# Attention probabilities left unscaled: row sums from a ones column of the values, spread by a matmul, and new orders on three engines

## The chip, the cores and the metric

The kernel runs on 1 NeuronCore of one Trainium2 chip. The metric is the device time of one execution in microseconds (us).

## The reference, cut to what matters

Four small transformer blocks act on one image of 16 x 16 = 256 tokens with 192 channels: three relative-position attention blocks (numbers 0, 1, 2), one causal attention block (number 3), and five mixture-of-experts blocks between and behind them. Each attention has 12 heads of 16 channels. Block 0, cut:

```python
attn = einsum('bnqd,bnkd->bnqk', q * scale, k) + rel_h[..., None] + rel_w[..., None, :]
attn = softmax(attn, axis=-1)                      # 12 heads x 256 queries x 256 keys
out = einsum('bnqk,bnkd->bnqd', attn, v)           # 16 channels a head
return einsum('bhwc,oc->bhwo', out, proj_w) + proj_b
```

Block 3 has no relative positions and a causal mask: the first 128 queries see only the first 128 keys.

## The kernel before

Five engines run their own written-out lists of instructions; semaphores alone join them, and each engine executes its list strictly in order. The blocks follow each other (`BLOCKS`); every block waits for the one before it, since each works on the whole of `x`.

In an attention block (`attn(n)` on each engine) TensorE first makes queries, keys and values. In blocks 0 to 2 the relative-position products go to DRAM and come back gathered (`rel`), and VectorE copies them into `q_st`. TensorE then transposes `k_st` (line 743) and `q_st` (line 760); between the two stand some matmuls on constant data, `stay_warm` (line 672), whose result nobody reads.

The heads then go in six pairs, p = 0 to 5. This is the pair loop:
- `scores(p)` (TensorE, line 777) writes two heads' 256 x 256 scores into two PSUM banks. There are two sets of banks, so pair p uses those of pair p - 2.
- `row_max(p)` (VectorE, line 1196; in block 3 a mask is added first and lines 1189 and 1192 take its place) makes the negated row maxima, one instruction a head.
- `exps(p)` (ScalarE, line 537) writes exp(score - max) to `probs`, two instructions a head, each with a row sum as a second output (`accum_out`).
- `recip(p, h)` (VectorE, line 1200) inverts the row sums, 2 numbers per partition.
- GpSimd (line 432) multiplies `probs` of one head, 128 x 512, by them. The very first head of a block is scaled by VectorE instead (line 1207).
- `probs_transposed(p)` (TensorE, line 805) makes 8 transposes into two banks; ScalarE copies one (line 550), VectorE the other (line 1218), to `pT`.
- For each of three groups of four heads, `values_summed(g)` (TensorE, line 817) multiplies by the values `v_st`, whose heads are padded from 16 to 32 columns with zeros; ScalarE copies the result to `oT` (line 544), and `project(g)` (line 786) applies the output projection.

When the last projection is done VectorE adds the result to `x` (line 1226), and the layer norm of the next block begins. TensorE's order of scores, transposes, value sums and projections is a loop over p, as are ScalarE's and VectorE's.

```python
                        for t in range(TT):
                            act.activation(probs[:, p % 2, h, t, 0:keys_of(n, t)], scores_bank(p, h)[:, t, 0:keys_of(n, t)], ACT.Exp,
                                           bias=nmax[:, p % 2, h, t:t + 1],
                                           accum_out=rsum[:, p % 2, h, t:t + 1]).then_inc(exp_ready, 1)
```

Of the kernel before, what the change touches and what calls it, by code (L numbers as in the profile page):

```python
# [13 lines left out]
P = 128  # L14
SIDE = 16
T = SIDE * SIDE
TT = T // P
# [56 lines left out]
def metaformer_kernel(nc, a, out):  # L74

    ctx = ExitStack()
    with ctx:
# [36 lines left out]
        yplace = sb("yplace", [P, C])  # L114
        nmax = sb("nmax", [P, 2, 2, TT])
        rsum = sb("rsum", [P, 2, 2, TT])
        rinv = sb("rinv", [P, 2, 2, TT])
# [90 lines left out]
        rinv_ready, p_ready, p_ready_dve = sem("rinv_ready"), sem("probs_ready"), sem("probs_ready_dve")  # L208
# [188 lines left out]
        def _(pool):  # L397
# [10 lines left out]
            pool.memset(v_st[:, :, :, :], 0.0).then_inc(pool_ready, 1)  # L408
# [12 lines left out]
            def attn(n):  # L421
                if not ATTN[n]["rel"]:


                    pool.wait_ge(qT_psum, 3 * n)
                    pool.memset(q_st[:, :, :, HD:HD + 2 * SIDE], 0.0).then_inc(q_clear, 1)
                for p in range(PAIRS):
                    g = n * PAIRS + p
                    for h in range(1 if p == 0 else 0, 2):
                        pool.wait_ge(rinv_ready, 2 * g + h + 1)  # L430
                        pr = probs[:, p % 2, h]
                        pool.tensor_tensor(pr, pr, rinv[:, p % 2, h].unsqueeze(2).broadcast_to([P, TT, T]), ALU.mult).then_inc(p_ready, 1)  # L432
# [56 lines left out]
        def _(act):  # L489
# [19 lines left out]
            def attn(n):  # L509
# [7 lines left out]
                if n == 0:  # L517
                    act.wait_ge(pool_ready, 4)
# [14 lines left out]
                def exps(p):  # L533
                    for h in range(2):
                        act.wait_ge(nmax_ready, 2 * (n * PAIRS + p) + h + 1)
                        for t in range(TT):
                            act.activation(probs[:, p % 2, h, t, 0:keys_of(n, t)], scores_bank(p, h)[:, t, 0:keys_of(n, t)], ACT.Exp,  # L537
                                           bias=nmax[:, p % 2, h, t:t + 1],
                                           accum_out=rsum[:, p % 2, h, t:t + 1]).then_inc(exp_ready, 1)

                def outputs(g):

                    act.wait_ge(o_psum, n * GROUPS + g + 1)
                    act.activation(oT[:, g, :], bank[B_O[g]][:, 0:T], ACT.Copy).then_inc(o_ready, 1)
# [3 lines left out]
                for p in range(PAIRS):  # L548
                    act.wait_ge(pT_psum, n * PAIRS + p + 1)
                    act.activation(pT[:, p % 3, 0].rearrange("p h t -> p (h t)"), bank[B_PT[0]][:, :], ACT.Copy).then_inc(pT_act, 1)  # L550
                    if p + 2 < PAIRS:
                        exps(p + 2)
                    if p and p % 2 == 0:
                        outputs(p // 2 - 1)
                outputs(GROUPS - 1)
# [96 lines left out]
        def _(pe):  # L652
# [21 lines left out]
            def attn(n, k):  # L674
# [73 lines left out]
                stay_warm(3 if n < 3 else 0, B_V)  # L748
# [15 lines left out]
                def scores(p):  # L764
# [7 lines left out]
                    if p == 4:  # L772
                        pe.wait_ge(qT_act, 2 * n + 2)

# [18 lines left out]
                def probs_transposed(p):  # L793
# [4 lines left out]
                    for h in range(2):  # L798
                        if p == 0 and h == 0:
                            pe.wait_ge(p_ready_dve, n + 1)  # L800
                        else:
                            pe.wait_ge(p_ready, (2 * PAIRS - 1) * n + 2 * p + h)
# [18 lines left out]

                pe.wait_ge(qT_dve, n + 1)
                stay_warm(2 if n == 3 else 1, B_PT[0])

                for p in range(PAIRS):
                    if p == 0:
                        probs_transposed(0)
                        scores(2)
                        pe.wait_ge(qT_act, 2 * n + 2)
                        continue  # L830
                    if p + 2 < PAIRS:
                        pe.wait_ge(p_ready, (2 * PAIRS - 1) * n + 2 * p + 1)
                        scores(p + 2)
                    probs_transposed(p)
                    if p % 2 == 0:
                        values_summed(p // 2 - 1)
                    if p == PAIRS - 2:
# [672 lines left out]
```

## Time and profile before

| | |
|---|---|
| time, median of 3 runs | 487.48 us (485.43 to 493.93) |
| the profiled execution | 492.98 us |
| span of its trace, first to last instruction | 491.1 us |
| TensorE busy | 439.6 us, 90% |
| VectorE busy | 339.2 us, 69% |
| ScalarE busy | 234.6 us, 48% |
| GpSimd busy | 173.5 us, 35% |
| mean granted TensorE clock | 0.983 of 2.4 GHz |

PE is TensorE, DVE is VectorE, ACT is ScalarE, POOL is GpSimd. The profiled execution is 1.9 us longer than its span. Busy shares are over the whole kernel, most of which is expert blocks; what an edit of the attention is worth must be read from the stretches of the four pair loops. A row gives start and duration in us (durations marked ns are nanoseconds), the engine, the line of the kernel, and, in brackets, how long the engine stood idle before it and what ended that. TensorE's matmuls overlap, so the distance between two starts is what one costs, not its duration. A 32-bit matmul shows as two records. A row of windows has the stretch, its length, the busy us of PE, PEld (weight loads), DVE, ACT and POOL, each with its count, then the granted clock, the DMA share and GB/s.

### The profile page before, as it was taken

What the parts mean: (1) busy time and instruction counts of PE and PEld (TensorE: products, weight loads), DVE (VectorE), ACT (ScalarE), POOL (GpSimd) and SP (SyncE); (2) the same over time, 40 slices, a digit from 0 to 9 for tenths busy, and PEclk for the clock granted to TensorE, in tenths of its full rate; (3) what the DMA queues carried; (4) which work ended last, traced back from release to release, by engine and by line L of the source; (5) the groups of instructions that cost most, each with busy time, mean ns of one, the idle gap of its engine ahead of it and who ended that gap; (6) DMA issues with size and microseconds to landing.
All of it is one profiled execution on the core that took longest, in us unless ns stands there. A gap on an engine that the chain in (4) does not pass through costs nothing.

```text
span 491.1 us, 9136 instructions
## 1 busy us (share of the span) xinstructions
PE 439.6 (90%) x3184; PEld 377.4 (77%) x3184; DVE 339.2 (69%) x780; ACT 234.6 (48%) x591; POOL 173.5 (35%) x171
## 2 busy tenths in 40 slices
PE   7968899999878889999877778799989999989997
PEld 5745799998555789998655555555679999979997
DVE  3664898996464798997456466441189899878764
ACT  1376456542266576552158146422237655537442
POOL 5044465652044446643026105310045576400000
PEclk9989999999989999999989997999999999999999
DMA  5840145620570045530489300702214655524551
GB/s 151 289 93 1 62 125 216 192 81 3 194 230 1 25 154 191 184 123 1 132 237 277 93 0 1 193 2 109 116 59 126 218 184 173 182 88 166 185 185 35
DMA packets 19364, 62.38 MB, mean 127 GB/s; under 512 B 4041, under 2 KB 6914, under 8 KB 19330
## 3 DMA queue, kind: packets, MB, share of 16 engines
q1 hardware_dynamic: 19330, 61.93, 39.7%
q8 instruction: 21, 0.34, 0.3%
q14 instruction: 13, 0.11, 0.1%
HBM read 59.82 MB, written 2.10 MB: 126 GB/s over the span
## 4 chain that ended last, share of the span: by engine, by line
PE 66%; issue 11%; DVE 10%; POOL 5%; DMA 4%; ACT 3%; SPq 1%; POOLq 0%; DVEq 0%
PE bank L966 25%; PE bank L974 10%; PE bank L986 7%; PE bank L777 4%; PE bank L988 4%; POOL probs L432 3%; PE bank L805 3%; DVE nmax L1196 2%; ACT probs L537 2%; DMA rel<-rel_scratch 2%; POOL rstd L400 2%; PE bank L760 1%; PE bank L672 1%; PE bank L817 1%; PE bank L711 1%
## 5 line engine op out<-in xcount | busy, mean ns | idle before, releaser
L966 PE MATMUL bank<-xT_hi,w_hi 128*128 128x256 f32 x408 | 109.1, 289 | 1.6 <-issue 1.6
L1234 DVE TENSOR_TENSOR w_lo<-w,w_hi 128x512 fp32r<-128x512 f32 x102 | 97.8, 996 | 2.1
L611 ACT ACTIVATE hid<-bank,b 128x256 f32<-128x256 f32 x150 | 62.8, 472 | 68.5 <-PE bank L966 68.4
L966 PE MATMUL bank<-xT_hi,w_lo 128*128 128x256 f32 x408 | 81.9, 282 | 0.0
L966 PEld LDWEIGHTS bank<-xT_hi,w_hi 128*128 128x128 f32 x408 | 77.8, 191 | 3.9 <-issue 3.8
L432 POOL TENSOR_TENSOR probs<-probs,rinv 128x512 f32<-128x512 f32 x44 | 44.9, 1041 | 96.1 <-DVE rinv L1200 96.0
L451 POOL TENSOR_TENSOR w_hl<-w,consts 128x384 fp32r<-128x384 f32 x50 | 52.5, 1050 | 74.4 <-PE bank L988 70.7
L966 PEld LDWEIGHTS bank<-xT_hi,w_lo 128*128 128x128 f32 x408 | 63.4, 191 | 0.0
L453 POOL TENSOR_TENSOR w_hl<-w,w_hl 128x384 fp32r<-128x384 f32 x50 | 58.9, 1179 | 3.9
L974 PE MATMUL bank<-w,hid 128*128 128x192 f32 x308 | 56.3, 327 | 3.3 <-issue 3.3
L563 ACT ACTIVATE w_hi<-w 128x512 fp32r<-128x512 f32 x102 | 58.4, 627 | 0.0
L966 PE MATMUL bank<-xT_lo,w_hi 128*128 128x256 f32 x204 | 57.6, 283 | 0.0
L986 PE MATMUL bank<-w_hl,hid_hi 128*128 128x384 f32 x176 | 54.3, 374 | 0.0
L974 PEld LDWEIGHTS bank<-w,hid 128*128 128x128 f32 x308 | 49.3, 190 | 4.5 <-issue 3.9
L988 PE MATMUL bank<-w_hl,hid_lo 128*128 128x192 f32 x200 | 50.7, 253 | 0.0
L537 ACT ACTIVATE probs<-bank,nmax 128x256 f32<-128x256 f32 (+1 forms) x96 | 43.0, 462 | 14.7 <-DVE nmax L1196 8.8
L672 PE MATMUL bank<-warm 128*128 128x256 f32 x168 | 43.0, 395 | 1.2 <-DVE warm L1385 1.2
L805 PE MATMUL bank<-consts,probs 128*128 128x128 f32 x180 | 26.9, 290 | 15.3 <-DVE pT L1218 6.7
L966 PEld LDWEIGHTS bank<-xT_lo,w_hi 128*128 128x128 f32 x204 | 39.0, 191 | 0.0
L805 PEld LDWEIGHTS bank<-consts,probs 128*128 128x128 f32 x180 | 20.5, 146 | 23.5 <-DVE probs L1207 7.7
L988 PEld LDWEIGHTS bank<-w_hl,hid_lo 128*128 128x128 f32 x200 | 38.2, 191 | 0.0
L777 PE MATMUL bank<-kT,qT 64*128 64x256 f32 (+1 forms) x192 | 29.3, 446 | 7.9 <-POOL probs L432 7.9
(167 smaller groups left out, 677.5 us busy)
## 6 DMA issues: line engine op xcount, KB each, us to landing
w<-in_M_w_dram SPq DMA_DIRECT2D x34, 768.0 KB, 5.4
w<-in_M_w_dram SPq DMA_DIRECT2D x33, 576.0 KB, 4.0
w<-in_M_w_dram SPq DMA_DIRECT2D x9, 288.0 KB, 2.7
wqkv<-in_A_wqkv_dram SPq DMA_DIRECT2D x4, 432.0 KB, 7.0
rel_scratch<-relall SPq DMA_DIRECT2D x4, 372.0 KB, 2.3
wproj<-in_A_wproj_dram SPq DMA_DIRECT2D x4, 288.0 KB, 8.4
wqkv<-in_M_w_dram SPq DMA_DIRECT2D x2, 576.0 KB, 21.7
rel<-rel_scratch SPq DMA_DIRECT2D x10, 96.0 KB
```

What stands on the lines that cost most here:

```text
L432: pool.tensor_tensor(pr, pr, rinv[:, p % 2, h].unsqueeze(2).broadcast_to([P, TT, T]), ALU.mult).then_inc(p_ready, 1)
L451: pool.tensor_tensor(parts[:, :, 0], w, one, ALU.mult).then_inc(w2_hi_ready, 1)
L453: pool.tensor_tensor(parts[:, :, 1], w, parts[:, :, 0].bitcast(F32), ALU.subtract).then_inc(w2_lo_ready, 1)
L537: act.activation(probs[:, p % 2, h, t, 0:keys_of(n, t)], scores_bank(p, h)[:, t, 0:keys_of(n, t)], ACT.Exp, bias=nmax[:, p % 2, h, t:t + 1 ...
L563: act.activation(w1_cols(w1_hi, b), w1_cols(w1[s], b), ACT.Copy).then_inc(w1_hi_ready, 1)
L611: ins = act.activation(hid[:, 2 * b + c, :], bank[B_H[b]][:, c * T:(c + 1) * T], FUNC[cfg["act"]], bias=b1[:, kb, bass.ds(at, 1)])
L805: ins = pe.transpose(bank[B_PT[kt]][:, h * T + t * P:h * T + (t + 1) * P], probs[:, p % 2, h, t, kt * P:(kt + 1) * P], ident)
L966: ins = pe.matmul(bank[B_H[b]][:, c2 * T:(c2 + 1) * T], w, xs, start=(q == 0), stop=(q == 4))
L974: ins = pe.matmul(bank[B_Y[t]][:, 0:C], hid[:, c, t * P:(t + 1) * P], w2[s][:, c * C:(c + 1) * C], start=(c == 0), stop=(c == nc2 - 1), sk ...
L986: pe.matmul(out[:, 0:2 * C], hid_hi[:, c, tok], w2_hl[:, c].rearrange("p a n -> p (a n)"), start=False, stop=(c == SC - 1), skip_group_che ...
L988: ins = pe.matmul(out[:, 0:C], hid_lo[:, c, tok], w2_hl[:, c, 0], start=False, stop=(c == SC - 1), skip_group_check=True)
L1234: dve.tensor_tensor(w1_cols(w1_lo, b), w1_cols(w1[s], b), w1_cols(w1_hi, b).bitcast(F32), ALU.subtract)\
```

## The change

The probabilities keep their exponentials as they are. Column 16 of each head's 32 value columns becomes 1 instead of 0, so that `values_summed` also gives, in row 16 of each head's 32 rows of output, the sum of that head's exponentials for every query. ScalarE copies the unscaled result to `oT`; a new matmul with a constant matrix of zeros and ones (`spread`) writes each head's sum into all 32 of its rows in the other half of the same PSUM bank (`sums_spread`); VectorE inverts this 128 x 256 array into `inv` and multiplies `oT` by it (`scaled`); only then may `project` start. The row sums of the exponentials, their inversions, all scaling by GpSimd and the one by VectorE are gone. GpSimd builds `spread` once.

The orders of the pair loop on TensorE, ScalarE and VectorE are written out anew. The numbers of `stay_warm` matmuls change: ahead of the query transposes from 3, 3, 3, 0 to 3, 6, 7, 0 for blocks 0 to 3, and between `scores(1)` and the first transposes of probabilities from 1, 1, 1, 2 to 3 everywhere. `scores(p)` for p of 2 and more now waits for the exponentials of pair p - 2, which free its banks.

The diff without declarations:

```diff
@@ -405,7 +405,8 @@
             ln(0)
             pool.wait_ge(xn_ready, TT)
             pool.memset(k_st[:, :, :, :], 0.0).then_inc(pool_ready, 1)
-            pool.memset(v_st[:, :, :, :], 0.0).then_inc(pool_ready, 1)
+            pool.memset(v_st[:, :, :, HD:HD + 1], 1.0).then_inc(pool_ready, 1)
+            pool.memset(v_st[:, :, :, HD + 1:], 0.0).then_inc(pool_ready, 1)
             pool.memset(kT[:, :, :], 0.0).then_inc(pool_ready, 1)
             pool.memset(gates[:, :, E:E + 1], 1.0).then_inc(pool_ready, 1)
             pool.wait_ge(c_in, 16)
@@ -419,17 +420,14 @@
                 pool.tensor_copy(q_st[:, t, :, HD + SIDE:HD + 2 * SIDE], oh).then_inc(kst_ready, 1)
 
             def attn(n):
+                if n == 0:
+                    pool.tensor_copy(spread[:, :].rearrange("p (b r) -> p b r", r=32),
+                                     consts[:, HD:P:32].unsqueeze(2).broadcast_to([P, 4, 32])).then_inc(spread_ready, 1)
                 if not ATTN[n]["rel"]:
 
 
                     pool.wait_ge(qT_psum, 3 * n)
                     pool.memset(q_st[:, :, :, HD:HD + 2 * SIDE], 0.0).then_inc(q_clear, 1)
-                for p in range(PAIRS):
-                    g = n * PAIRS + p
-                    for h in range(1 if p == 0 else 0, 2):
-                        pool.wait_ge(rinv_ready, 2 * g + h + 1)
-                        pr = probs[:, p % 2, h]
-                        pool.tensor_tensor(pr, pr, rinv[:, p % 2, h].unsqueeze(2).broadcast_to([P, TT, T]), ALU.mult).then_inc(p_ready, 1)
 
             def split(m, j, i):
 
@@ -515,7 +513,7 @@
                                        bank[B_REL[2 * t + 1]][:, 0:offsets * NH // 2].rearrange("p (r n) -> p r n", n=NH // 2),
                                        ACT.Copy).then_inc(rel_act, 1)
                 if n == 0:
-                    act.wait_ge(pool_ready, 4)
+                    act.wait_ge(pool_ready, 5)
                     for i in range(4):
                         act.wait_ge(kw_psum, i + 1)
                         act.activation(kw_rows(i, 0), kw_bank(i, HD + SIDE), ACT.Copy).then_inc(kw_act, 1)
@@ -535,24 +533,32 @@
                         act.wait_ge(nmax_ready, 2 * (n * PAIRS + p) + h + 1)
                         for t in range(TT):
                             act.activation(probs[:, p % 2, h, t, 0:keys_of(n, t)], scores_bank(p, h)[:, t, 0:keys_of(n, t)], ACT.Exp,
-                                           bias=nmax[:, p % 2, h, t:t + 1],
-                                           accum_out=rsum[:, p % 2, h, t:t + 1]).then_inc(exp_ready, 1)
+                                           bias=nmax[:, p % 2, h, t:t + 1]).then_inc(exp_ready, 1)
 
                 def outputs(g):
 
                     act.wait_ge(o_psum, n * GROUPS + g + 1)
-                    act.activation(oT[:, g, :], bank[B_O[g]][:, 0:T], ACT.Copy).then_inc(o_ready, 1)
+                    act.activation(oT[:, g, :], bank[B_O[g]][:, 0:T], ACT.Copy).then_inc(o_raw, 1)
+
+                def turned(p):
+                    act.wait_ge(pT_psum, n * PAIRS + p + 1)
+                    act.activation(pT[:, p % 3, 0].rearrange("p h t -> p (h t)"), bank[B_PT[0]][:, :], ACT.Copy).then_inc(pT_act, 1)
 
                 exps(0)
                 exps(1)
-                for p in range(PAIRS):
-                    act.wait_ge(pT_psum, n * PAIRS + p + 1)
-                    act.activation(pT[:, p % 3, 0].rearrange("p h t -> p (h t)"), bank[B_PT[0]][:, :], ACT.Copy).then_inc(pT_act, 1)
-                    if p + 2 < PAIRS:
-                        exps(p + 2)
-                    if p and p % 2 == 0:
-                        outputs(p // 2 - 1)
-                outputs(GROUPS - 1)
+                turned(0)
+                exps(2)
+                turned(1)
+                exps(3)
+                turned(2)
+                outputs(0)
+                exps(4)
+                turned(3)
+                exps(5)
+                turned(4)
+                outputs(1)
+                turned(5)
+                outputs(2)
 
             def split(m, j, i, b):
 
@@ -745,7 +751,7 @@
                     ins.then_inc(kT_psum, 1)
 
                 pe.wait_ge(v_ready, n + 1)
-                stay_warm(3 if n < 3 else 0, B_V)
+                stay_warm((3, 6, 7, 0)[n], B_V)
                 if n == 0:
                     pe.wait_ge(kw_act, 4)
                     pe.wait_ge(kw_dve, 4)
@@ -771,6 +777,8 @@
                         pe.wait_ge(qT_dve, n + 1)
                     if p == 4:
                         pe.wait_ge(qT_act, 2 * n + 2)
+                    if p >= 2:
+                        pe.wait_ge(exp_ready, 4 * (n * PAIRS + p - 1))
 
                     for t in range(TT):
                         for h in range(2):
@@ -796,10 +804,7 @@
                         pe.wait_ge(pT_act, n * PAIRS + p)
                         pe.wait_ge(pT_dve, n * PAIRS + p)
                     for h in range(2):
-                        if p == 0 and h == 0:
-                            pe.wait_ge(p_ready_dve, n + 1)
-                        else:
-                            pe.wait_ge(p_ready, (2 * PAIRS - 1) * n + 2 * p + h)
+                        pe.wait_ge(exp_ready, 4 * (n * PAIRS + p) + 2 * (h + 1))
                         for t in range(TT):
                             for kt in range(keys_of(n, t) // P):
                                 ins = pe.transpose(bank[B_PT[kt]][:, h * T + t * P:h * T + (t + 1) * P],
@@ -819,27 +824,35 @@
                                             stop=(kt == TT - 1), skip_group_check=(n == 3))
                     ins.then_inc(o_psum, 1)
 
+                def sums_spread(g):
+
+                    if n == 0 and g == 0:
+                        pe.wait_ge(spread_ready, 1)
+                    pe.wait_ge(o_raw, GROUPS * n + g + 1)
+                    pe.matmul(bank[B_O[g]][:, T:2 * T], spread[:, :], oT[:, g, :], start=True, stop=True).then_inc(osum_psum, 1)
+
                 pe.wait_ge(qT_dve, n + 1)
-                stay_warm(2 if n == 3 else 1, B_PT[0])
-
-                for p in range(PAIRS):
-                    if p == 0:
-                        probs_transposed(0)
-                        scores(2)
-                        pe.wait_ge(qT_act, 2 * n + 2)
-                        continue
-                    if p + 2 < PAIRS:
-                        pe.wait_ge(p_ready, (2 * PAIRS - 1) * n + 2 * p + 1)
-                        scores(p + 2)
-                    probs_transposed(p)
-                    if p % 2 == 0:
-                        values_summed(p // 2 - 1)
-                    if p == PAIRS - 2:
-                        project(0)
-                    if p == PAIRS - 1:
-                        project(1)
-                values_summed(GROUPS - 1)
-                project(GROUPS - 1)
+                stay_warm(3, B_PT[0])
+
+                probs_transposed(0)
+                scores(2)
+                scores(3)
+                probs_transposed(1)
+                scores(4)
+                probs_transposed(2)
+                values_summed(0)
+                probs_transposed(3)
+                scores(5)
+                probs_transposed(4)
+                sums_spread(0)
+                values_summed(1)
+                probs_transposed(5)
+                project(0)
+                values_summed(2)
+                sums_spread(1)
+                sums_spread(2)
+                project(1)
+                project(2)
 
             def places():
 
@@ -1120,7 +1133,7 @@
                             .then_inc(qTs_ready, 1)
                     settle()
                 if n == 0:
-                    dve.wait_ge(pool_ready, 5)
+                    dve.wait_ge(pool_ready, 6)
                 def values():
                     dve.wait_ge(v_psum, TT * (n + 1))
                     for t in range(TT):
@@ -1195,30 +1208,36 @@
                         else:
                             dve.tensor_reduce(nmax[:, p % 2, h, :], scores_bank(p, h), AX.X, ALU.max, negate=True).then_inc(nmax_ready, 1)
 
-                def recip(p, h):
-                    dve.wait_ge(exp_ready, 4 * (n * PAIRS + p) + 2 * (h + 1))
-                    dve.reciprocal(rinv[:, p % 2, h], rsum[:, p % 2, h]).then_inc(rinv_ready, 1)
-
-                row_max(0)
-                row_max(1, 0)
-                recip(0, 0)
-                dve.wait_ge(rinv_ready, 2 * n * PAIRS + 1)
-                pr = probs[:, 0, 0]
-                dve.tensor_tensor(pr, pr, rinv[:, 0, 0].unsqueeze(2).broadcast_to([P, TT, T]), ALU.mult).then_inc(p_ready_dve, 1)
-                recip(0, 1)
-                row_max(1, 1)
-                for p in range(PAIRS):
-                    if p + 1 < PAIRS:
-                        for h in range(2):
-                            recip(p + 1, h)
-                    if p and p + 2 < PAIRS:
-                        row_max(p + 2)
+                def turned(p):
                     dve.wait_ge(pT_psum, n * PAIRS + p + 1)
                     first_q = P if n == 3 else 0
                     dve.tensor_copy(pT[:, p % 3, 1, :, first_q:T],
                                     bank[B_PT[1]][:, :].rearrange("p (h t) -> p h t", h=2)[:, :, first_q:T]).then_inc(pT_dve, 1)
-                    if p == 0:
-                        row_max(2)
+
+                def scaled(g):
+
+                    dve.wait_ge(osum_psum, GROUPS * n + g + 1)
+                    if n or g:
+                        dve.wait_ge(o_ready, GROUPS * n + g)
+                    dve.reciprocal(inv[:, :], bank[B_O[g]][:, T:2 * T]).then_inc(inv_ready, 1)
+                    dve.wait_ge(inv_ready, GROUPS * n + g + 1)
+                    dve.tensor_tensor(oT[:, g, :], oT[:, g, :], inv[:, :], ALU.mult).then_inc(o_ready, 1)
+
+                row_max(0)
+                row_max(1)
+                turned(0)
+                row_max(2)
+                row_max(3)
+                turned(1)
+                row_max(4)
+                turned(2)
+                turned(3)
+                row_max(5)
+                scaled(0)
+                turned(4)
+                turned(5)
+                scaled(1)
+                scaled(2)
                 settle()
                 at = []
                 for t in range(TT):
```

## Rows read from the trace of the kernel before

**Rows 1.** windows over the four pair loops

```profile
23.10:49.10 26.00, 19.93 (x159) 14.13 (x159) 13.91 (x32) 17.16 (x60) 11.20 (x11) 0.93 0.28 64
135.10:160.60 25.50, 20.02 (x159) 14.05 (x159) 13.93 (x33) 17.29 (x60) 11.20 (x11) 0.93 0.36 110
249.50:274.50 25.00, 18.97 (x159) 13.29 (x159) 13.63 (x32) 17.69 (x59) 11.20 (x11) 0.99 1.00 279
288.50:315.40 26.90, 18.77 (x149) 13.01 (x149) 16.52 (x57) 15.88 (x58) 11.28 (x11) 0.87 0.31 81
```

**Rows 2.** the chain that ended last, in block 1's pair loop: start, us, what

```profile
144.91 2.05 POOL probs L432 x2
```

**Rows 3.** timeline of PE in block 1's pair loop

```profile
147.00 1.13 PE L777 MATMUL bank<-kT,qT 64*128 64x256 f32 x8 [1.45 <-POOL probs L432]
148.07 1.09 PE L805 MATMUL bank<-consts,probs 128*128 128x128 f32 x8
149.09 1.07 PE L817 MATMUL bank<-pT,v_st 128*32 128x256 f32 x16
...
153.71 1.06 PE L805 MATMUL bank<-consts,probs 128*128 128x128 f32 x8 [1.46 <-DVE pT L1218]
154.70 1.07 PE L817 MATMUL bank<-pT,v_st 128*32 128x256 f32 x16
...
159.89 0.92 PE L786 MATMUL bank<-wproj,oT 128*128 128x192 f32 x4 [0.49 <-ACT oT L544]
```

**Rows 4.** timeline of ACT: an expert block, then block 1's pair loop

```profile
73.21 0.84 ACT L611 ACTIVATE hid<-bank,b 128x256 f32<-128x256 f32 x2 [0.94 <-PE bank L966]
...
149.20 0.60 ACT L550 ACTIVATE pT<-bank 128x512 f32<-128x512 f32 x1 [0.90 <-PE bank L805]
149.69 0.47 ACT L537 ACTIVATE probs<-bank,nmax 128x256 f32<-128x256 f32 x1
150.05 0.20 ACT L537 ACTIVATION_READ_ACCUMULATOR probs<-bank,nmax 128x1 f32 x1
150.15 0.48 ACT L537 ACTIVATE probs<-bank,nmax 128x256 f32<-128x256 f32 x1
...
155.84 0.38 ACT L544 ACTIVATE oT<-bank 128x256 f32<-128x256 f32 x1 [0.43 <-PE bank L817]
```

**Rows 5.** timeline of DVE in block 1's pair loop

```profile
145.66 1.27 DVE L1196 TENSOR_REDUCE nmax<-bank 128x2 f32<-128x512 f32 x2
146.84 0.68 DVE L1218 COPY pT<-bank 128x512 f32<-128x512 f32 x1
```

**Rows 6.** timeline of DVE in block 3's pair loop, one head

```profile
297.09 0.43 DVE L1189 TENSOR_TENSOR bank<-bank,consts 128x256 f32<-128x256 f32 x1 [1.15 <-PE bank L777]
...
298.09 0.42 DVE L1189 TENSOR_TENSOR bank<-bank,consts 128x256 f32<-128x256 f32 x1
```

**Rows 7.** single lines of DVE: duration min/median/max ns, first and last start

```profile
L1200 DVE RECIPROCAL rinv<-rsum x48: 154/166/167, 26.0 to 310.0; 128x2 f32<-128x2 f32 x48
L1246 DVE TENSOR_TENSOR logits<-bank,rbias x2: 163/170/176, 169.2 to 438.9; 128x16 f32<-128x16 f32 x2
L1302 DVE TENSOR_TENSOR hid<-silu_g,bank x27: 410/422/422, 440.9 to 486.9; 128x256 f32<-128x256 f32 x27
```

**Rows 8.** windows around stretches of low clock, columns as in group 1

```profile
137.00:140.30 3.30, 1.39 (x9) 0.75 (x7) 2.80 (x7) 3.30 (x15) 1.13 (x2) 1.00 1.04 329
140.90:144.30 3.40, 3.40 (x17) 2.44 (x16) 2.01 (x4) 1.28 (x4) 1.31 (x2) 0.51 0.86 224
301.30:304.60 3.30, 3.10 (x18) 2.12 (x22) 2.65 (x11) 1.83 (x8) 1.96 (x3) 0.51 0.02 5
```

**Rows 9.** timeline of PE ahead of the pair loops of blocks 1 and 2

```profile
133.61 1.53 PE L760 MATMUL bank<-consts,q_st 128*128 128x128 f32 x12 [1.35 <-DVE q_st L1174]
...
243.20 1.46 PE L672 MATMUL bank<-warm 128*128 128x256 f32 x6
246.72 2.81 PE L760 MATMUL bank<-consts,q_st 128*128 128x128 f32 x12 [2.06 <-DVE q_st L1174]
```

More of the change, by code:

```diff
@@ L114, in metaformer_kernel @@
         yplace = sb("yplace", [P, C])
+        inv = sb("inv", [P, T])
+        spread = sb("spread", [P, P])
         nmax = sb("nmax", [P, 2, 2, TT])
-        rsum = sb("rsum", [P, 2, 2, TT])
-        rinv = sb("rinv", [P, 2, 2, TT])
         warm = sb("warm", [P, T])
@@ L207, in metaformer_kernel @@
         s_psum, nmax_ready, exp_ready = sem("scores_psum"), sem("nmax_ready"), sem("exp_ready")
-        rinv_ready, p_ready, p_ready_dve = sem("rinv_ready"), sem("probs_ready"), sem("probs_ready_dve")
+        spread_ready, o_raw, osum_psum, inv_ready = sem("sum_spreader_ready"), sem("o_unscaled_copied"), sem("o_sums_psum"), sem("o_sums_inverted")
         pT_psum, pT_dve, pT_act = sem("pT_psum"), sem("pT_dve"), sem("pT_act")
```

## The prediction, made before the changed kernel was run

> **What bounds the kernel now.** I read first the busy shares by engine, then windows laid over the four pair loops, then the chain of waits inside them, then each engine's timeline in block 1's loop, which blocks 0 and 2 repeat. The page says TensorE is busy 90% of the span, but that is the mean with the expert blocks, which the change leaves alone. Over the pair loops TensorE is busy 19 to 20 of 25 to 27 us, ScalarE 16 to 18, VectorE 14 to 17, GpSimd 11 [rows 1]: no engine is full, so a loop is a chain that walks between engines. GpSimd's scaling of two heads, 2.05 us, stands on that chain [rows 2], and TensorE's scores, which need its banks back, stood idle 1.45 us for it [rows 3]. The four loops last 26.0, 25.5, 25.0 and 26.9 us, 103.4 together, a fifth of the span. Only here and just ahead can the change act.
>
> **The slots.** From start to start a pair's scores cost TensorE 1.07 us, eight transposes 1.02 (I take 1.05 for both) and a group's value sums, 16 records in 1.07, about 1.00; from the start of value sums to the start of ScalarE's copy of them it is 1.14 (154.70 to 155.84), and the last projection at 159.89 lets VectorE update `x` at 160.6, 0.70 later [rows 1, 3, 4]. On ScalarE an exponential costs 0.46 (149.69 to 150.15), with the reading of the row sum in it; the expert block's ACTIVATE of the same 128x256 shape, also with a bias per partition but no sum, repeats after 0.84 - 0.47 = 0.37 [rows 4]. So each exponential loses 0.09, a pair 0.36. A turned pair's copy costs 0.49 before the next instruction can start. On VectorE a head's maxima cost 0.59, a turned copy 0.68 until done [rows 5]; in block 3 a head costs 1.00 [rows 6].
>
> **What is removed.** 44 multiplications on GpSimd (11 a block), four on VectorE, 48 small inversions. Nothing takes over GpSimd's place in a pair: transposes wait for the exponentials directly. What is late next is ScalarE: four exponentials of 0.37 and a copy of 0.49 are 1.97 us a pair, TensorE's scores, transposes and value sums 2.60, so TensorE should be the fullest, with waits where the written order makes it wait.
>
> **What is added.** Per group a 128x256 matmul; the same shape on constant data costs 0.43 (six records in 1.46, the last lasting 0.38, so 0.216 a record) [rows 9]. I give it 0.65 until its reader starts. Then a reciprocal of 128x256 from PSUM and a multiplication of 128x256 on VectorE. The trace has no reciprocal of that size. The low end is any VectorE operation on 128x256, 0.42. For the high end: a reciprocal of 2 elements lasts 166 ns and a sum of 16 elements 170 ns [rows 7], so up to eight steps per element could hide under the fixed part. An element's step is (0.68 - 0.42)/256 = 1.0 ns [rows 5, 7], and 256 x 8 steps with a fixed 0.16 make 2.2 us. I take 0.44, since the small reciprocal is the nearest row and is not longer than its neighbours. Multiplying costs 0.33 of slot and 0.47 until done. The wait inside `scaled(0)` holds up VectorE's turned copies of pairs 4 and 5 queued behind it, and TensorE waits for these.
>
> The Trainium skill has both answers. "VectorE: DVE Perf Modes", section "First, the fixed hardware budget", says that the reciprocal is an iterative divide with a repeat count of 8; if that means eight steps per element, the sum is that of the second rival. "Vector Engine (DVE) Microarchitecture Reference", section "3.2 Anatomy of a single slice", says that the chain of divide steps spans all eight slices, which reads like a pipeline that takes an element a step, and the sum is the forecast's. The small rows exclude neither.
>
> **The new loop, step by step,** counted from the first scores. Two scores and three `stay_warm` matmuls: 3.4. Transposes 0, scores 2 and 3, transposes 1: 7.6. Scores 4 wait for the exponentials of pair 2, that ScalarE starts when pair 2's maxima are there: 7.8. Scores 4, transposes 2, then value sums of group 0 until ScalarE starts their copy: 11.0. ScalarE: that copy 0.28, exponentials of pair 4 1.48, turned copy of pair 3 0.67: 13.4. Transposes 4 and the first spreading matmul: 15.1. VectorE: reciprocal, multiplication, turned copy of pair 4 (0.44 + 0.33 + 0.76): 16.7. Transposes 5 until their readers start 1.10, turned copy 0.76: 18.5. Value sums of group 2 and ScalarE's copy 1.14 + 0.44: 20.1. VectorE is then still on group 1 until 20.9; reciprocal and multiplication of group 2: 21.8. Last projection 0.70: 22.5 us. The tail has grown: from the last transposes to the end are now 5.8 us, with VectorE steps in it that the old order did not have. Block 3, with 1.00 a head for maxima but shorter scores and transposes, comes to 22.6 by the same steps.
>
> The same bookkeeping applied to the old order, GpSimd with 1.0 us a head, gives 24.1 at full clock, against 25.5 measured in block 1. The rest is the clock. TensorE is at 0.51 for 3.4 us there (and for as long in block 3), which costs 1.7 us of work; the level of 1.2 GHz came right after 3.3 us in which TensorE was busy 1.39 [rows 8]. That hole is where it waited for the first pair's maxima, exponentials and scaling. In the new order three `stay_warm` matmuls (1.29) run up to the first transposes, and the longest idle piece I find is 0.8 us. So I count full clock throughout. The Trainium skill, "TensorE: Matmul & The Clock Gate", section "HAM oscillation — how this bites in real kernels", holds that idle gaps bring the low clock back; by that rule, the trace agrees.
>
> Ahead of block 2's loop the query transposes take 2.81 us against 1.53 in block 1, at the low clock, after TensorE sat idle 2.06 us for the gathered `rel` [rows 9]. Four more `stay_warm` matmuls cost 4 x 0.43 = 1.7 and end at about 246.4, before the 246.72 at which `q_st` is ready: they cost nothing and I expect the 1.3 back. In block 1 three more (1.3) fit the 1.35 of idle time just so; if the cover fails they cost a few tenths.
>
> **The sum.** Block 0: 26.0 - 22.5 = 3.5. Block 1: 25.5 - 22.5 = 3.0. Block 2: 25.0 - 22.5 + 1.3 = 3.8. Block 3: 26.9 - 22.6 = 4.3. Together 14.6 us. The profiled execution would go from 492.98 to 478.4 and its span from 491.1 to 476.5. The median of the runs is 5.5 us under the profiled execution; taken off there, 487.48 - 14.6 = 472.9. About 2% is what a measurement of this kernel can tell from no change: below 477.7 counts as faster, above 497.2 as slower.
>
> **Rivals.** First, the clock falls all the same. The new loop still has waits of TensorE (before scores 4, transposes 4 and 5, the last two projections), most of all in block 3, where VectorE's 2.0 us a pair starve it. Then only the difference at full clock is left: 24.1 - 22.5 = 1.6 in three loops and 2.4 in block 3, 7.2 together: 487.48 - 7.2 = 480.3. For it speaks that block 3 fell twice before; against it, that every new gap is far shorter than the holes that preceded a fall [rows 8].
>
> Second, on the other side: the reciprocal takes 2.2 us. It stands on the chain three times a loop (once ahead of turned copy 4, twice in the tail, where TensorE has nothing else to do), so each loop grows by 3 x 1.8 = 5.4 to about 27.9, 21.6 us in all: 472.9 + 21.6 = 494.5, and idle tails that long could bring the low clock, some 3 us more. The point from which it decides: 14.6 us over 12 reciprocals is 1.2, so at 1.6 us each the change is worth nothing. For it speaks only that the small rows allow it; against it, that a reciprocal of 2 is 4 ns shorter than its neighbour of 16, which leaves exactly no room beyond eight steps.
>
> Third, the change does not shorten the chain as it says, since the old waits for GpSimd partly covered those for maxima and copies: every pair keeps its period and only clock and start improve, about 5 to 8 us: 480 to 482. ScalarE's and VectorE's shorter slots speak against it.
>
> **How the numbers follow.** Forecast 0.62, clock 0.13, slow reciprocal 0.17, no shorter chain 0.08. The forecast's own range is 469 to 477: two us for my slots of 0.65 and 0.44, two for tenths in the clock. 467 to 484 takes in the clock and the third rival and leaves out the reciprocal's 0.17. Faster by over 2%: most of the forecast and a part of the clock case, 0.66. Slower by over 2%: half of the slow reciprocal, 0.10. The rest is within, 0.24.
>
> **What would show it.** Right: RECIPROCAL 128x256 at about 0.4 us; ACTIVATE of exponentials every 0.37; granted clock 1.00 over all four loops and over block 2's query transposes; loops of 22 to 23 us; the end of a loop on the chain as VectorE's scaling, not GpSimd. Wrong: a reciprocal over 1.6 us, which turns the sign; windows at 0.50 in the loops; or TensorE idle a microsecond and more ahead of transposes 4 and 5.

## The result and the profile after

The changed kernel takes 500.15 us (median of 4 runs, 497.77 to 501.82) against 487.81 (485.43 to 493.93) for the kernel before in the same job: a ratio of 1.022, 95% interval 1.0167 to 1.0273, so slower by 12.3 us between the medians, 8 to 13 us by the interval, where 14.6 us faster was forecast. The profiled execution took 501.82, its span 500.0.

The page after, the busy line and the granted clock in 40 slices (tenths, 9 is 90% or more):

```profile
PE 457.3 (91%) x3236; PEld 391.8 (78%) x3236; DVE 355.2 (71%) x752; ACT 224.2 (45%) x495; POOL 128.8 (26%) x129
...
PEclk9998899999998799999998799799999999999999
```

GpSimd has lost its work in the loops (11.20 to 0.00 us in each of blocks 0 to 2), but VectorE has gained 4.5 to 4.8 us in each of them. Windows over the four loops, over stretches of block 1's and over one microsecond of block 0's tail (columns as in [rows 1]: PE, PEld, DVE, ACT, POOL, granted clock, DMA share, GB/s):

```profile
22.70:50.20 27.50, 21.91 (x169) 15.76 (x169) 18.49 (x26) 15.54 (x37) 0.00 (x0) 0.94 0.25 63
136.80:165.60 28.80, 22.66 (x169) 15.93 (x169) 18.46 (x26) 15.54 (x37) 0.00 (x0) 0.89 0.32 97
252.80:281.60 28.80, 22.62 (x169) 15.90 (x169) 18.46 (x26) 15.27 (x35) 0.00 (x0) 0.89 0.96 245
295.80:323.20 27.40, 19.15 (x157) 13.15 (x157) 20.88 (x50) 13.26 (x34) 0.00 (x0) 0.94 0.30 87
...
150.00:153.00 3.00, 2.53 (x26) 1.54 (x26) 2.39 (x3) 2.41 (x7) 0.00 (x0) 1.00 0.00 0
153.00:155.00 2.00, 0.20 (x2) 0.23 (x3) 1.67 (x3) 0.30 (x1) 0.00 (x0) 1.00 0.00 0
157.00:159.00 2.00, 2.00 (x17) 0.73 (x16) 0.00 (x0) 0.13 (x1) 0.00 (x0) 0.50 0.03 8
164.00:166.00 2.00, 1.64 (x5) 1.64 (x6) 0.66 (x2) 0.00 (x0) 0.00 (x0) 0.50 0.00 0
...
47.00:48.00 1.00, 1.00 (x4) 0.66 (x3) 1.00 (x1) 0.00 (x0) 0.00 (x0) 0.50 0.00 0
```

Measured from the first scores to the start of the addition into `x` (into `tln` in block 3), the loops last 27.3, 28.7, 28.7 and 27.2 us; by the same two marks those of before lasted 26.0, 25.5, 25.0 and 26.9. The forecast was 22.5 and 22.6. What fills VectorE is one line. All instructions that write or read `inv`, duration in ns as min/median/max:

```profile
L1222 DVE RECIPROCAL inv<-bank x12: 1746/1758/1758, 37.8 to 319.7; 128x256 f32<-128x256 f32 x12
L1224 DVE TENSOR_TENSOR oT<-oT,inv x12: 424/425/426, 39.6 to 321.5; 128x256 f32<-128x256 f32 x12
```

The reciprocal of 256 elements per partition takes 1.76 us, four times the 0.44 that I had taken. VectorE's timeline in block 1's loop shows its three places: one ahead of the turned copy of pair 4, and two in the tail, back to back:

```profile
151.88 1.76 DVE L1222 RECIPROCAL inv<-bank 128x256 f32<-128x256 f32 x1 [0.61 <-PE bank L832]
153.67 0.42 DVE L1224 TENSOR_TENSOR oT<-oT,inv 128x256 f32<-128x256 f32 x1
154.02 0.68 DVE L1214 COPY pT<-bank 128x512 f32<-128x512 f32 x1
159.77 1.76 DVE L1222 RECIPROCAL inv<-bank 128x256 f32<-128x256 f32 x1 [3.17 <-PE bank L832]
161.56 0.42 DVE L1224 TENSOR_TENSOR oT<-oT,inv 128x256 f32<-128x256 f32 x1
162.09 1.76 DVE L1222 RECIPROCAL inv<-bank 128x256 f32<-128x256 f32 x1
163.88 0.42 DVE L1224 TENSOR_TENSOR oT<-oT,inv 128x256 f32<-128x256 f32 x1
```

TensorE's timeline of the same stretch shows who waits for them:

```profile
150.32 1.09 PE L810 MATMUL bank<-consts,probs 128*128 128x128 f32 x8 [0.36 <-ACT pT L545]
151.25 0.60 PE L832 MATMUL bank<-oT,spread 128*128 128x256 f32 x2
151.78 1.07 PE L822 MATMUL bank<-pT,v_st 128*32 128x256 f32 x16
154.80 1.06 PE L810 MATMUL bank<-consts,probs 128*128 128x128 f32 x8 [1.96 <-issue]
155.70 1.23 PE L794 MATMUL bank<-wproj,oT 128*128 128x192 f32 x4
156.86 1.94 PE L822 MATMUL bank<-pT,v_st 128*32 128x256 f32 x16
158.73 1.43 PE L832 MATMUL bank<-oT,spread 128*128 128x256 f32 x4
162.04 0.95 PE L794 MATMUL bank<-wproj,oT 128*128 128x192 f32 x4 [1.88 <-DVE oT L1224]
164.36 1.65 PE L794 MATMUL bank<-wproj,oT 128*128 128x192 f32 x4 [1.36 <-DVE oT L1224]
```

Three holes, 1.96, 1.88 and 1.36 us, each ended by VectorE. The first is booked as "issue", because the profile has no releaser for it, but the copy of 154.02 ends at 154.70 and the transposes that wait for it start at 154.80. The holes cost a second time. In 153 to 155 us TensorE is busy 0.20 of 2.00, still at full clock; from 157 to 159 the granted clock is 0.50, the lower level of 1.2 GHz. The same 16 records of value sums take 1.07 us at 151.78 and 1.94 at 156.86; the same four projections 0.95 and 1.65. In blocks 0 and 3 the clock held longer. The hole ahead of the last transposes lasted 1.96 us in block 0 and 2.65 in block 3, and the value sums behind it still took 1.07 and 0.86, what they had taken ahead of it; the level of 1.2 GHz came only with the second hole, by 47 us in block 0. TensorE's timeline in block 3:

```profile
314.28 0.85 PE L810 MATMUL bank<-consts,probs 128*128 128x128 f32 x6 [2.65 <-DVE pT L1214]
```

The chain that ended last runs through block 1's stretch by the same steps (start, us, what):

```profile
152.85 1.96 issue
154.80 1.06 PE bank L810 x8
155.87 1.07 PE bank L794 x4
156.93 1.87 PE bank L822 x16
158.80 0.95 PE bank L832 x2
159.77 1.77 DVE inv L1222
162.09 1.77 DVE inv L1222
```

Where [rows 2] had GpSimd's scaling on the chain, it now has VectorE's reciprocals, as the second rival described.

### The profile page after: what moved, and what is told of

Read it like the earlier page. It is cut to its first block, busy times and chain, and to the rows that moved or that the text cites. A ratio compares the mean times of both kernels' runs of the same rounds, so it can differ in the third digit from the quotient of the medians.

```text
span 500.0 us, 9086 instructions
## 1 busy us (share of the span) xinstructions
PE 457.3 (91%) x3236; PEld 391.8 (78%) x3236; DVE 355.2 (71%) x752; ACT 224.2 (45%) x495; POOL 128.8 (26%) x129
## 4 chain that ended last, share of the span: by engine, by line
PE 72%; DVE 10%; issue 9%; DMA 4%; ACT 3%; SPq 1%; POOL 1%; DVEq 0%; POOLq 0%
PE bank L979 25%; PE bank L987 10%; PE bank L999 7%; PE bank L678 6%; PE bank L1001 4%; DVE inv L1222 3%; PE bank L785 3%; PE bank L810 3%; PE bank L822 3%; PE bank L794 2%; ACT probs L535 2%; DMA rel<-rel_scratch 2%; PE bank L766 1%; PE bank L717 1%; PE bank L956 1%
## 5 line engine op out<-in xcount | busy, mean ns | idle before, releaser
L1253 DVE TENSOR_TENSOR w_lo<-w,w_hi 128x512 fp32r<-128x512 f32 x102 | 96.2, 980 | 2.1
L400 POOL TENSOR_TENSOR rstd<-var_eps,minus_half 128x2 f32<-128x2 f32 x10 | 8.4, 841 | 224.4 <-DVE var_eps L1092 224.4
L678 PE MATMUL bank<-warm 128*128 128x256 f32 x196 | 56.7, 439 | 1.2 <-DVE warm L1404 1.2
L678 PEld LDWEIGHTS bank<-warm 128*128 128x128 f32 x196 | 42.4, 226 | 8.7 <-issue 1.3
L535 ACT ACTIVATE probs<-bank,nmax 128x256 f32<-128x256 f32 (+1 forms) x96 | 36.7, 471 | 10.3 <-DVE nmax L1209 5.9
L1329 DVE TENSOR_TENSOR hid_lo<-hid,hid_hi 128x512 fp32r<-128x512 f32 x50 | 34.6, 692 | 1.7
L810 PE MATMUL bank<-consts,probs 128*128 128x128 f32 x180 | 24.7, 278 | 11.3 <-issue 7.1
```

What stands on the lines that cost most here:

```text
L678: pe.matmul(bank[b][:, 0:T], warm[:, 0:P], warm[:, :], start=True, stop=True)
L810: ins = pe.transpose(bank[B_PT[kt]][:, h * T + t * P:h * T + (t + 1) * P], probs[:, p % 2, h, t, kt * P:(kt + 1) * P], ident)
L1253: dve.tensor_tensor(w1_cols(w1_lo, b), w1_cols(w1[s], b), w1_cols(w1_hi, b).bitcast(F32), ALU.subtract)\
```

## The experiments

The theory after the result: the new orders are sound, and the reciprocal's length alone turns the sign, by itself (12 x 1.32 = 16 us) and through the clock in the tails. The rivals: the new orders of the engines are themselves longer, or the clock is lost elsewhere.

**e1, the division replaced by a copy.** It leaves out the division: the value sums are multiplied by the row sums.

```
-dve.reciprocal(inv[:, :], bank[B_O[g]][:, T:2 * T]).then_inc(inv_ready, 1)
+dve.tensor_copy(inv[:, :], bank[B_O[g]][:, T:2 * T]).then_inc(inv_ready, 1)
```

> The changed kernel with the 12 reciprocals of 128x256 replaced by copies of the same shape; it leaves out the division, so values are not normalised. Theory: the reciprocal's length and what it does to the clock are the whole loss. A copy of 128x256 takes 0.42 us against 1.76, three times a loop on the chain: 12 x 1.34 = 16 us less; and with tails that short the granted clock should stay at 1.00, some 6 us more: 500.2 - 22 = 478 us. Rival A, the clock falls in the tail anyway: 484. Rival B, the spreading matmul and the waits around it cost most: over 490.

Measured 479.40, ratio to before 0.9806 (0.9755 to 0.9856), and the granted clock of its profile 1.000 over the whole span. The instruction in the reciprocal's place, and the window over block 1's loop:

```profile
L1222 DVE COPY inv<-bank x12: 414/425/425, 37.9 to 300.1; 128x256 f32<-128x256 f32 x12
132.74:155.66 22.92, 20.70 (x169) 14.77 (x169) 14.33 (x26) 15.54 (x37) 0.00 (x0) 1.00 0.38 111
```

Every other instruction, wait and order is that of the changed kernel, so 500.15 - 479.40 = 20.7 us hang on the length of 12 instructions. (The two were measured in different jobs; by their ratios to before, 1.022 - 0.9806, it is 20.2.) Its loops last 22.92 us each, where I had worked out 22.5 and 22.6. 12 x (1.758 - 0.425) = 16.0 are the direct part; 4.7 remain.

**e2, no normalising at all.** It leaves out the division by the row sums, with its spreading matmul and multiplication; projections wait for the copy of the value sums.

```
-act.activation(oT[:, g, :], bank[B_O[g]][:, 0:T], ACT.Copy).then_inc(o_raw, 1)
+act.activation(oT[:, g, :], bank[B_O[g]][:, 0:T], ACT.Copy).then_inc(o_ready, 1)
-sums_spread(0)    # likewise 1 and 2
-scaled(0)         # likewise 1 and 2
```

> The changed kernel with no spreading matmul, reciprocal or multiplication at all; the division of the softmax is left out, the new orders stay. Theory: the new order itself is sound; by the slots of the prediction a loop takes 20.2 us (21.1 in block 3) instead of about 28.3, so 500.2 - 31 = 469 us. Rival, the new order is at fault: it stays over 487.8, the kernel before.

Measured 469.00, ratio 0.9623 (0.9548 to 0.9698), loops 20.3 to 20.9, clock 1.000. Normalising by this route costs 31 us, 21 of them for the reciprocal instead of a copy and 10 for all the rest.

**e7, the old orders without scaling.** The kernel before, with its multiplications by the inverse row sums left out; transposes wait for the exponentials.

```
-pool.tensor_tensor(pr, pr, rinv[:, p % 2, h].unsqueeze(2).broadcast_to([P, TT, T]), ALU.mult).then_inc(p_ready, 1)
...
-pe.wait_ge(p_ready, (2 * PAIRS - 1) * n + 2 * p + h)
+pe.wait_ge(exp_ready, 4 * (n * PAIRS + p) + 2 * (h + 1))
```

> The kernel before with no scaling of the probabilities by GpSimd or VectorE (the division of the softmax is left out), old orders. Theory: in the old orders the scaling stood on the chain only in part; by the same slots a loop falls from 24.2 to 23.3 us: 487.8 - 4 = 484 us, some 3 less if the clock holds. Rival: GpSimd's 2.05 us a pair were fully on the chain: 487.8 - 4 x 6 = 464.

Measured 484.28, ratio 0.9901 (0.9863 to 0.9938). Leaving out the scaling, GpSimd's and VectorE's, is by itself worth 5 us. Neither this kernel nor e2 scales anything, yet 484.3 - 469.0 = 15 us lie between them: the rest of the change (orders, no row sums on ScalarE and no small inversions of them, warm matmuls) is where the gain sits. No run parts the orders from the missing row sums, but e6 below has the new orders with the row sums kept and is at 475.1.

**e3, the changed kernel with the old numbers of warm matmuls.**

```
-stay_warm((3, 6, 7, 0)[n], B_V)
+stay_warm(3 if n < 3 else 0, B_V)
-stay_warm(3, B_PT[0])
+stay_warm(2 if n == 3 else 1, B_PT[0])
```

> The changed kernel with the numbers of stay_warm matmuls of before (3, 3, 3, 0 and 1, 1, 1, 2). Theory: the added ones bought full clock up to the fourth transposes and over block 2's query transposes; without them the granted clock falls there again and the time rises by 1.3 + about 1 us a loop to some 504 us. Rival: they do nothing, or lengthen the tail's low clock: 500 or below.

Measured 498.44, ratio 1.0207 (1.0149 to 1.0265), not the 504 of the theory. The added warm matmuls buy nothing in the changed kernel: its loops last 27.0, 27.1, 28.6 and 27.2 without them. The query transposes ahead of block 2's loop, which I had said were slow for want of four of them, take 1.53 us here too:

```profile
247.32 1.53 PE L766 MATMUL bank<-consts,q_st 128*128 128x128 f32 x12 [0.72 <-DVE q_st L1187]
```

**e4, the old kernel with the new numbers,** the reverse of e3's diff on the kernel before.

> The kernel before with the changed kernel's numbers of stay_warm matmuls (3, 6, 7, 0 and 3 everywhere), nothing else. Theory: the clock's share of the hoped gain can be had alone: block 2's query transposes 1.3 us, and the low clock inside the loops 1.4 to 1.7 us each: 487.8 - 6 = 482 us. Rival: the waits for GpSimd's scaling keep the holes and the clock falls as before: 486.5, only block 2's share.

Measured 487.79 (10 runs), ratio 0.9979 (0.9946 to 1.0012): nothing that can be told from no change, and not the 482 of the theory. Its profiled execution had a span of 485.5 and loops of 24.6, 24.6, 24.8 and 26.7, so they ran 0.1 to 1.4 us shorter than in the profile of before, at the same median. The profile of before, 492.98, was one of its longer executions.

**e9, half the reciprocal.** The division reaches only the first 128 of 256 queries; the rest are multiplied by 1.

```
-dve.reciprocal(inv[:, :], bank[B_O[g]][:, T:2 * T]).then_inc(inv_ready, 1)
+dve.reciprocal(inv[:, 0:P], bank[B_O[g]][:, T:T + P]).then_inc(inv_ready, 1)
...
+then(dve.memset(inv[:, :], 1.0))    # once, ahead of the blocks
```

> The changed kernel with each reciprocal over 128 of the 256 queries; the other half is multiplied by one, so half of the division is left out. Theory: 0.95 us instead of 1.76 three times a loop, 12 x 0.81 = 9.7 us less, and between nothing and 4.7 us for the clock: 486 to 490.5, most likely 487 with the clock mostly held. Rival: the cost is a fixed wait per reciprocal and not its length: 498 to 500.

Measured 486.23 (10 runs), ratio 0.9934 (0.9902 to 0.9965), loops 24.4 to 24.8, each reciprocal 0.96 us. With 0.42, 0.96 and 1.76 us in this place the kernel takes 479.4, 486.2 and 500.2: 6.8 us for the first 0.53, where 12 x 0.53 = 6.4 is direct, and 14.0 for the next 0.80, where 9.6 is direct. The excess over the direct part comes mostly once the holes are long.

**e8, the changed kernel with its tail kept busy,** 12 warm matmuls a block in the three holes.

```
 values_summed(1)
+stay_warm(4, B_PROJ[0])
 probs_transposed(5)
...
 sums_spread(2)
+stay_warm(5, B_WARM)
 project(1)
+stay_warm(3, B_WARM)
 project(2)
```

> The changed kernel with stay_warm matmuls in the three places where TensorE stands idle for the reciprocals: 4 ahead of transposes 5, 5 ahead of project(1), 3 ahead of project(2), on free banks. Theory: of the 20.7 us between the changed kernel and the one with copies, 16.0 are the reciprocals themselves and some 4.7 the low clock that the idle tail brings; only these come back: 500.2 - 4.7 = 495.5 us, clock near 1.00. Rival: the clock costs nothing on the chain and the reciprocals delay the tail in another way: 499 to 501.

Measured 495.17, ratio 1.014 (1.0089 to 1.0191), loops 26.92 each, clock 1.000. Timeline of TensorE in block 1, and the window over its loop:

```profile
151.87 1.99 PE L678 MATMUL bank<-warm 128*128 128x256 f32 x8
...
162.12 0.92 PE L794 MATMUL bank<-wproj,oT 128*128 128x192 f32 x4
135.90:162.82 26.92, 25.76 (x193) 19.27 (x193) 18.33 (x26) 15.54 (x37) 0.00 (x0) 1.00 0.36 108
```

The projections that took 1.65 take 0.92. This is the clock's share, 500.15 - 495.17 = 5.0 us, and it agrees with the 4.7 left over from e1. Its size is rough: the two ratios, each known to half a per cent, give 3.9, and the loops of the two profiles 111.9 - 107.6 = 4.3. From e8 to e1 it is 15.8, against the direct 16.0, and each loop is 26.92 - 22.92 = 4.0 longer, three reciprocals' worth of 1.33: the difference between e1 and the changed kernel closes.

**e5, the disputed price by itself.** The kernel before, with reciprocals and copies of several sizes added behind the last work, from SBUF (`warm`) and from PSUM (`bank`).

```
+for cols in (4, 8, 16, 32, 64, 128, 256):
+    settle(); then(dve.reciprocal(probs[:, 0, 0, 0, 0:cols], warm[:, 0:cols]))
+...
```

> The kernel before with 14 VectorE instructions added at its end, each after the one before is done: reciprocals of 4, 8, 16, 32, 64, 128 and 256 elements a partition from SBUF, copies of 4, 16, 64 and 256, and reciprocals of 64, 256 and 512 from PSUM; nothing reads them. Theory: a reciprocal is a fixed part of 0.15 us plus 6.3 ns an element, wherever it reads from: 0.17, 0.20, 0.25, 0.35, 0.55, 0.95, 1.76 us and 0.55, 1.76, 3.4; copies 1.0 ns an element. Rival: the 1.76 us belongs to the PSUM operand, and from SBUF 256 elements take 0.42.

One run, 497.90. Groups by form on VectorE (busy us, mean ns of one):

```profile
L1415 DVE RECIPROCAL xn<-bank 128x512 f32<-128x512 f32 x1 | 3.4, 3357 | 0.0
L1415 DVE RECIPROCAL xn<-bank 128x256 f32<-128x256 f32 x1 | 1.8, 1758 | 0.0
L1409 DVE RECIPROCAL probs<-warm 128x256 f32<-128x256 f32 x1 | 1.8, 1753 | 0.0
L1409 DVE RECIPROCAL probs<-warm 128x64 f32<-128x64 f32 x1 | 0.6, 553 | 0.0
L1412 DVE COPY probs<-warm 128x256 f32<-128x256 f32 x1 | 0.3, 293 | 0.0
L1409 DVE RECIPROCAL probs<-warm 128x8 f32<-128x8 f32 x1 | 0.2, 203 | 0.0
L1409 DVE RECIPROCAL probs<-warm 128x4 f32<-128x4 f32 x1 | 0.2, 178 | 0.0
L1412 DVE COPY probs<-warm 128x4 f32<-128x4 f32 x1 | 0.2, 169 | 0.0
```

From 4 to 256 elements the reciprocal grows by 1753 - 178 = 1575 ns, 6.25 per element, with 153 fixed, wherever the source lies (3357 for 512 from PSUM fits: 153 + 3200). At 2 elements that line gives 166 ns, the very row on which I rested the cheap price [rows 7], while a copy of 4 takes 169. A row of 2 elements carries 12 ns of the slope. The copies grew by 0.49 ns per element from SBUF, not by the 1.0 that I had expected.

The additions stand behind the last work, so up to there this is a second profile of the kernel before. Its loops last 24.6, 25.1, 26.1 and 26.8 us, and its query transposes ahead of block 2's loop ran at full clock:

```profile
242.54 1.53 PE L760 MATMUL bank<-consts,q_st 128*128 128x128 f32 x12 [0.61 <-DVE q_st L1174]
```

**e6, invert first, then turn.** A version with the full division: ScalarE's exponentials write row sums as before; VectorE inverts a group's sums while they still lie 8 to a partition; GpSimd repeats each 32 times, TensorE turns them with the identity, ScalarE copies them to `inv`, and VectorE multiplies the value sums straight from PSUM. Orders otherwise as in the changed kernel.

```
-dve.reciprocal(inv[:, :], bank[B_O[g]][:, T:2 * T])
-dve.tensor_tensor(oT[:, g, :], oT[:, g, :], inv[:, :], ALU.mult)
+dve.reciprocal(rinv[:, :, 4 * g:4 * g + 4], rsum[:, :, 4 * g:4 * g + 4])
+pool.tensor_copy(rspread[...], rinv[:, :, 4 * g:4 * g + 4].unsqueeze(3).broadcast_to([P, TT, 4, 32]))
+pe.matmul(bank[9 - B_O[g]][:, T + t * P:T + (t + 1) * P], rspread[:, t], ident, start=True, stop=True)
+act.activation(inv[:, :], bank[9 - B_O[g]][:, T:2 * T], ACT.Copy)
+dve.tensor_tensor(oT[:, g, :], bank[B_O[g]][:, 0:T], inv[:, :], ALU.mult)
```

> The changed kernel's orders, but the row sums come from the exponentials' second output as before, VectorE inverts 8 of them per partition and group, GpSimd repeats each 32 times, TensorE turns them by a product with the identity, ScalarE copies them out and VectorE multiplies the value sums straight from PSUM. The division is done in full. Theory: no long reciprocal is on the chain; by the slots of the prediction a loop takes 21.7 to 22 us: 487.8 - 17 = 471 us, clock at 1.00. Rival: the longer path through four engines is late for the value sums, or the exponentials at 0.46 us bind: 480 and over.

Measured 475.12 (8 runs), ratio 0.9703 (0.9675 to 0.9731): faster than both kernels, by 14.5 us against before. Its three instructions for the inverses, from the views of `rinv` and `inv`:

```profile
L1235 DVE RECIPROCAL rinv<-rsum x12: 190/193/204, 31.1 to 295.4; 128x8 f32<-128x8 f32 x12
L434 POOL COPY rspread<-rinv x12: 396/400/401, 31.4 to 295.7; 128x256 f32<-128x256 f32 x12
...
L1231 DVE TENSOR_TENSOR oT<-bank,inv x12: 397/425/426, 35.2 to 298.8; 128x256 f32<-128x256 f32 x12
```

The division costs 0.19 us in place of 1.76, and the chain behind the value sums loses ScalarE's copy. Loops last 21.7 to 22.3, close to the 21.7 to 22 expected. They come to 87.9 together and e2's to 81.8, and 469.0 + 6.1 = 475.1. That the time is 4 us above the expected 471 has other grounds: the median of before was 489.4 in this job and not 487.8, and I had again counted the gain from the long profile of before and taken it off the median (next section).

## Why the prediction was wrong

**The step that failed** is the price in "What is added": "I take 0.44, since the small reciprocal is the nearest row and is not longer than its neighbours". The bounds of 0.42 and 2.2 us held the measured 1.76; the choice between them was wrong. The row of 2 elements was nearest in operation but lies 128 times away in size, and on the line found in e5 it says 12 ns of its 166 about the price per element. Its 4 ns below a sum of 16 did bound the price at about eight steps, and the truth is 6.25 ns, about six of the 1.0 ns steps. No row spoke for one step rather than six, so 0.17 for that rival was far too little. [rows 7] even allowed a better estimate, which I did not make: the sum of 16 elements (170 ns) and the product of 256 (422) lie on a line with a fixed part of 153 ns; with that, 2 elements in 166 ns are 6.4 ns each, and 256 of them 1.8 us. It would have been loose, since the 163 to 176 ns of the sum allow anything from 3 to 10 ns, but its middle was right. Of my two readings of the Trainium skill, eight steps per element from "VectorE: DVE Perf Modes" ("First, the fixed hardware budget") and one from "Vector Engine (DVE) Microarchitecture Reference" ("3.2 Anatomy of a single slice"), the measurement bears out neither, and lies near the first.

**The second rival was right in its mechanism.** Three reciprocals on each loop's chain, in the places it named, and low clock in the tails. By its own steps with 1.76 each loop grows by 3 x 1.32 = 4.0, 16 us in all, and the tails' low clock adds 4.7 to 5.0 in place of "some 3": 472.9 + 20.7 = 493.6. Its turning point of 1.6 us was too high: with 0.96 us the kernel is 0.7% faster than before and with 1.76 it is 2.2% slower, so a line between the two crosses at about 1.1. The gain in hand was e1's 9.5 us and not 14.6.

**The remaining 6.5 us** are what e1 lies above the forecast, 479.4 - 472.9. Of them 1.8 are not the change's: over the 13 runs in e1's job the kernel before has a median of 489.3, not 487.48. The loops at full clock last 22.92, not 22.5 and 22.6: 1.6 in the sum of four. The other 3.1 came from carrying the profile's differences over to the median. The bound of 24.1 for the old order at full clock was 0.5 short (24.6 in blocks 0 and 1 of e4's profile and in block 0 of e5's), but I counted the gain from the profile's 26.0, 25.5, 25.0, 26.9, and then took off the 5.5 us between profile and median a second time. e5's profile shows where most of the 5.5 lay: there the kernel's last work ends at 484.4 us, 4.5 earlier than in the profile of before (488.9). Only 0.8 of that are the loops (103.4 - 102.6). The other 3.8 lie between the loops of blocks 1 and 2 (88.9 against 85.1), where the idle time ahead of the query transposes was 0.61 in place of 2.06 and the transposes took 1.53 in place of 2.81. From e5's loops the gain of e1 is 102.6 - 91.7 = 10.9, from e4's 100.8 - 91.7 = 9.1, against 9.5 measured (0.0194 of 489.3). Which loops the median run of before had is inferred from these profiles.

**Clock and warm matmuls.** "I count full clock throughout" holds until the first hole: the fall of [rows 8] ahead of the first transposes is gone. It fails in the tail, where the holes come from the reciprocal; in e1 and e2 the clock is 1.000. The 1.3 us in block 2 appeared in the profile, 2.81 to 1.53 (timeline of TensorE, after):

```profile
248.00 3.19 PE L678 MATMUL bank<-warm 128*128 128x256 f32 x14
251.32 1.53 PE L766 MATMUL bank<-consts,q_st 128*128 128x128 f32 x12
```

but e3 has it without the added matmuls, e5 has it in the old kernel itself, and e4 gains nothing with them, so the step took one execution's low clock for a property of the kernel. Why it was low there stays open; the idle time ahead of it was 2.06 us, against 0.72 and 0.61 in e3 and e5 and 1.68 in e7, where the transposes took 1.53 as well.

**What held.** Exponentials repeat every 0.37 us instead of 0.46 (four in 1.60 with the last lasting 0.47). Transposes of pair 4 start at 150.32, 13.51 after the first scores at 136.81, where I had 13.4. Without the scaling transposes wait for the exponentials directly, which alone is worth 5 us (e7). The third rival, no shorter chain, falls with e1: its loops last 22.92 against 24.6 in the old order, both at full clock. But its 480 to 482 us are nearer to e1's 479.4 than the forecast's 472.9 is, so the orders by themselves gained less than I had forecast. The 0.65 us for the spreading matmul fits: 151.25 to 151.88 until its reader starts.

## What to carry to other kernels

A price per element can't be read by holding an instruction on 2 elements against its neighbours; take the fixed part off first, and see how loose the rest is. Where an operation is new at a size, give both ends real weight, and work out at what price the change turns before looking at the rest. Invert while a sum is one number per row, before it is spread or turned: on the chain the inversion then costs 0.19 us on 8 elements in place of 1.76 on 256 (e6), though GpSimd, TensorE and ScalarE then have to spread, turn and copy the result. Set a profile's gains against the median only after asking which of its losses the median run has; a second profile of the same kernel tells.

## What the runs showed of the hardware

The reciprocal on VectorE takes 153 ns + 6.25 ns per element of a partition, the same from SBUF and PSUM within 5 ns (e5), where a copy of 256 takes 293 ns from SBUF and 425 from PSUM. In the profile after, a hole of 1.96 us in TensorE's work, with matmuls on both sides of it, was followed by the 1.2 GHz level in block 1 (by 157 us), and so was one of 1.95 in block 2; in blocks 0 and 3 the clock stayed at 1.00 behind a first hole of 1.96 and 2.65 us and fell with the second. In e1's profile, without these holes, it never fell. Warm matmuls in the holes (e8) bought back 4 to 5 us and cost the chain nothing; the ones added elsewhere (e3, e4) bought nothing that could be measured. Executions of one kernel differ in this: block 2's query transposes of the old kernel took 2.81 us in one profile and 1.53 in another (before, e5).
